# Step sizes of a selective scan made ahead of the scan and kept in DRAM

## The chip, the cores and the metric

The kernel runs on one core of one Trainium2 chip, as one program. The metric is its time on the device in microseconds (us). A core has five engines that run side by side and meet only at semaphores: PE (TensorE, matmul), DVE (VectorE, elementwise and scans), ACT (ScalarE, activation functions), POOL (GpSimd, here elementwise too) and SP (SyncE, which here issues nearly all DMAs). SBUF is the memory in which the arrays lie (one large tensor, `arena`), PSUM (`ps`, eight banks of 512 float32 columns) is what PE writes, DRAM is outside. Each engine works through its own instructions in their written order.

## What is computed

The reference is one block: a group norm, a Mamba-like branch (convolution and a selective scan in four directions) that is added to x, an attention step without softmax, and a mixture of eight experts. The change touches the branch alone:

```python
B_, H_, W_, DM = (4, 32, 32, 384); DI = 192; N = 16; R = 24; K = 4      # 1024 positions per image
xz = _gn(x) @ in_proj_w.T
xh, z = jnp.split(xz, 2, axis=-1)
xc = silu(depthwise_conv3x3(xh) + conv_b)
xs = [xc by rows, xc by columns, and both reversed]                     # K = 4 directions
x_dbl = einsum('bkdl,kcd->bkcl', xs, x_proj_w)
dts, Bs, Cs = jnp.split(x_dbl, [R, R + N], axis=2)
dts = softplus(einsum('bkrl,kdr->bkdl', dts, dt_projs_w) + dt_projs_b)  # the delta of each channel and position
def step(h, inp):
    dA = jnp.exp(d_t[..., None] * As)
    h = h * dA + (d_t * u_t)[..., None] * B_t[:, :, None, :]
    y = jnp.einsum('bkcn,bkn->bkc', h, C_t)
out_y = selective_scan(xs, dts, As, Bs, Cs, Ds)
y = layernorm(sum of the four directions) * silu(z);  return y @ out_proj_w.T
```

## The kernel before

**Tiles.** The four images are worked on in two pairs (`NP` = 2). A tile is 128 partitions (64 channels of both images of a pair) by 1024 positions. There are twelve tiles q (`NQ`: 2 pairs, 2 orders, by rows and by columns, 3 groups of 64 channels), each with two directions, forwards and backwards. A tile and a direction together are a half (24 of them); a half has 16 units, one for each n of the state, so a tile has `UN` = 32 units, and there are 384 in all.

**Prologue.** A loop over the pairs: DVE takes the sums of the group norm of an image, PE adds them over groups and spreads them back, DVE normalises x, PE makes the input projection in three fills of two PSUM banks per image, ACT takes them out (xh into the padded image `xpad`, silu of z into `z_sb`). Then the convolution, three fills per pair: PE does 5 of 9 taps (`PE_TAPS`) with diagonal weights, DVE the other four in `tap_sum` and adds them, ACT applies silu into `xy`, POOL copies the result by columns. A second loop makes the projection `x_proj` for each direction k: ACT copies the rows, and DVE and ACT split B and C into three bfloat16 parts, which SP stores in DRAM (`bc_parts`, `b_rows`, `dt_rows`).

**Scan.** For each unit u: ACT makes the decay, exp(delta * a) (line 624). PE spreads row n of B over the partitions (line 838) and DVE multiplies that by delta * x (line 1235). For 6 of the 16 n (`ON_POOL`) POOL makes this input instead (line 457), from a row of B that SP loads broadcast from `b_rows` into a ring of `XRING` = 2. DVE scans (line 1242). PE spreads the row of C, ACT copies it out of PSUM (line 632), POOL multiplies the states of two units by it (line 476), and PE adds the products up in PSUM, five units later (`LAG`, line 857). At the end of a tile DVE takes the sum out (line 1212).

**The delta** of a half is made while the half ahead of it is scanned. After given n, PE multiplies the rows of dt (line 846), ACT takes it out of PSUM, then Abs, Exp, +1 and Ln (lines 594 to 609); DVE has three steps between them, after n = 7, 10 and 11 (`DELTA_AT`, lines 1195, 1200 and 1205: the part lost in rounding, max(x, 0) + log, and the difference); after n = 12 POOL makes delta * x (line 450, `delta_x`). Only the first half's delta is made ahead of the scan.

**Order.** All of it is written out by hand: what stands behind what in an engine's program, and waits on semaphores. Nothing reorders it. SP too works in order: it waits for what it stores and then issues.

After the scan come the norm over channels, the output projection, attention and the experts, which the change leaves as they are.

## Time and profile before

| | |
|---|---|
| median of 3 runs | 2713.69 us (2710.76 to 2716.58) |
| the profiled execution's own time | 2710.37 us |
| its span, first to last instruction | 2708.6 us |
| mean granted TensorE clock | 0.918 |
| up to the first scan | 0 to 267.22 us |
| scan, to the start of what follows it | 267.22 to 1654.31 us |
| the rest | 1654.31 to 2708.6 us |

In the stretch 260 to 1655 us, DVE is busy 1312.43 us of 1395, POOL 1316.03, PE 1110.14 and ACT 903.03. A busy time says that an instruction was running, not that it got on: an instruction that is held up inside counts as busy. Hence the same instruction is compared in places where its neighbours differ.

### The profile page before, as it was taken

What the parts mean: (1) busy time and instruction counts of PE and PEld (TensorE: products, weight loads), DVE (VectorE), ACT (ScalarE), POOL (GpSimd) and SP (SyncE); (2) the same over time, 40 slices, a digit from 0 to 9 for tenths busy, and PEclk for the clock granted to TensorE, in tenths of its full rate; (3) what the DMA queues carried; (4) which work ended last, traced back from release to release, by engine and by line L of the source; (5) the groups of instructions that cost most, each with busy time, mean ns of one, the idle gap of its engine ahead of it and who ended that gap; (6) DMA issues with size and microseconds to landing.
All of it is one profiled execution on the core that took longest, in us unless ns stands there. A gap on an engine that the chain in (4) does not pass through costs nothing.

```text
span 2708.6 us, 21624 instructions
## 1 busy us (share of the span) xinstructions
PE 2190.3 (81%) x6116; PEld 1001.7 (37%) x6116; DVE 1622.6 (60%) x1337; ACT 1152.9 (43%) x1277; POOL 1446.6 (53%) x503
## 2 busy tenths in 40 slices
PE   3886777788787887887878886679998469999998
PEld 1332233333332333333333332345545335555554
DVE  2433999999999999999999995632221200000000
ACT  1225666666666666666666662211111011211111
POOL 0001899999999999999999993000000321111110
PEclk9987899989999989999989988789999689999999
DMA  5115121212222222121122124001100342222230
GB/s 199 58 23 136 55 54 55 54 54 72 54 55 53 54 72 60 49 62 52 49 61 56 54 55 181 23 35 47 47 14 33 133 156 107 107 106 104 105 105 16
DMA packets 69131, 193.92 MB, mean 72 GB/s; under 512 B 10160, under 2 KB 35875, under 8 KB 67426
## 3 DMA queue, kind: packets, MB, share of 16 engines
q1 hardware_dynamic: 62946, 176.45, 21.3%
q0 software_dynamic: 6144, 16.98, 1.8%
q8 instruction: 19, 0.31, 0.0%
q14 instruction: 22, 0.18, 0.0%
HBM read 154.89 MB, written 40.44 MB: 72 GB/s over the span
## 4 chain that ended last, share of the span: by engine, by line
PE 46%; DVE 22%; issue 17%; POOL 8%; ACT 3%; DMA 1%; SPq 1%; DVEq 1%; POOLq 0%; ACTq 0%
PE ps L1093 9%; PE ps L1081 9%; DVE arena L1242 6%; PE ps L857 6%; DVE ps L1235 5%; POOL arena L476 5%; PE ps L801 3%; DVE arena L1200 3%; PE ps L1045 3%; DVE arena L1195 2%; PE ps L970 2%; PE ps L838 2%; POOL arena L450 2%; PE ps L812 2%; PE ps L846 2%
## 5 line engine op out<-in xcount | busy, mean ns | idle before, releaser
L476 POOL TENSOR_TENSOR arena<-arena 128x2048 f32<-128x2048 f32 x192 | 906.9, 4734 | 40.5 <-DVE arena L1242 39.1
L857 PE MATMUL ps<-arena 128*128 128x512 f32 x1536 | 792.5, 641 | 80.8 <-POOL arena L476 65.5
L1242 DVE TENSOR_TENSOR_SCAN arena<-arena,ps 128x1024 f32<-128x1024 f32 x240 | 548.7, 2286 | 40.9 <-DVE ps L1235 29.7
L632 ACT ACTIVATE arena<-ps 128x1024 f32<-128x1024 f32 x384 | 391.9, 1021 | 357.4 <-PE ps L838 352.4
L838 PE MATMUL ps<-arena 96*128 (+1 forms) x1248 | 375.1, 411 | 205.8 <-DVE arena L1242 165.0
L857 PEld LDWEIGHTS ps<-arena 128*128 128x128 f32 x1536 | 308.1, 204 | 375.0 <-issue 236.0
L457 POOL TENSOR_TENSOR arena<-arena 128x1024 f32<-128x1024 f32 x144 | 362.2, 2516 | 29.1 <-DMA arena<-b_rows 26.9
L1242 DVE TENSOR_TENSOR_SCAN arena<-ps,arena 128x1024 f32<-128x1024 f32 x144 | 327.2, 2272 | 11.1 <-ACT ps L624 10.9
L838 PEld LDWEIGHTS ps<-arena 96*128 96x128 bf16 x1248 | 116.0, 103 | 555.1 <-DVE arena L1242 248.3
L1235 DVE TENSOR_TENSOR ps<-ps,arena 128x1024 f32<-128x1024 f32 x240 | 290.9, 1212 | 20.1 <-PE ps L838 17.6
L1459 DVE TENSOR_TENSOR arena<-ps,arena 128x384 f32<-128x384 f32 x32 | 17.8, 557 | 448.9 <-PE ps L1093 448.9
L624 ACT ACTIVATE arena<-arena 128x1024 f32<-128x1024 f32 x240 | 273.7, 1141 | 2.6 <-DVE arena L1205 2.6
L514 POOL DMA_INDIRECT out<-arena x32 | 31.8, 993 | 435.8 <-DVE arena L1464 435.8
L492 POOL COPY arena<-arena 128x384 f32 x32 | 17.8, 597 | 454.4 <-DVE arena L1364 454.4
L1093 PE MATMUL ps<-arena 128*128 128x384 f32 x768 | 250.1, 486 | 0.0
L1081 PE MATMUL ps<-arena 128*128 128x512 f32 x576 | 248.7, 592 | 0.0
L624 ACT ACTIVATE ps<-arena 128x1024 f32<-128x1024 f32 x144 | 160.8, 1117 | 61.0 <-DVE arena L1242 60.6
L1093 PEld LDWEIGHTS ps<-arena 128*128 128x128 f32 x768 | 145.4, 190 | 101.6 <-issue 3.8
L1081 PEld LDWEIGHTS ps<-arena 128*128 128x128 f32 x576 | 109.6, 191 | 135.8 <-issue 134.0
L748 ACT ACTIVATE arena<-ps,arena 128x512 f32<-128x512 f32 x96 | 66.0, 688 | 175.9 <-PE ps L1081 175.9
L755 ACT ACTIVATE arena<-arena 128x384 f32<-128x384 f32 x32 | 16.7, 523 | 232.3 <-DVE arena L1459 232.3
L443 POOL COPY arena<-arena x6 | 12.4, 2071 | 174.2 <-ACT arena L561 174.2
(167 smaller groups left out, 1891.9 us busy)
## 6 DMA issues: line engine op xcount, KB each, us to landing
arena<-b_rows SPq DMA_DIRECT2D x288, 256.0 KB, 3.9
arena<-in_w SPq DMA_DIRECT2D x16, 2304.0 KB, 13.2
slot_in<-arena SPq DMA_DIRECT2D x8, 772.0 KB, 16.2
arena<-slot_in SPq DMA_DIRECT2D x8, 772.0 KB, 18.0
arena<-in_xT SPq DMA_DIRECT2D x4, 1536.0 KB, 9.4
arena<-in_x_tok SPq DMA_DIRECT2D x1, 6144.0 KB, 21.9
tokens<-arena SPq DMA_DIRECT2D x4, 1536.0 KB, 6.2
out<-arena SPq DMA_DIRECT2D x4, 1536.0 KB, 9.7
```

What stands on the lines that cost most here:

```text
L457: nc.gpsimd.tensor_tensor(xin[:, x % XRING], xin[:, x % XRING], dux[:, dr], ALU.mult).then_inc(in_ok, 1)
L476: nc.gpsimd.tensor_tensor(hst[:, h:h + 2], hst[:, h:h + 2], c_sb[:, c:c + 2], ALU.mult).then_inc(p2_ok, 2)
L624: nc.scalar.activation(dst, dlt[:, dr], ACT.Exp, scale=a_neg[:, q % OJ, dr, n:n + 1]).then_inc(dec_ok, 1)
L632: nc.scalar.activation(c_sb[:, u % RING], C_PS, ACT.Copy).then_inc(c_free, 1)
L801: mm = pe.matmul(SLOT3[n % 3][:, h * 512:(h + 1) * 512], w_in[:, t, r, j], xt[:, r, t, h * 512:(h + 1) * 512], start=(t == 0), stop=(t == ...
L838: mm = pe.matmul(dst[:, h * 512:(h + 1) * 512], sel_lhs[0:BR, n], bc[0:BR, q % OJ // J, dr, m, h * 512:(h + 1) * 512], start=True, stop=True)
L857: mm = pe.matmul(Y_PS[:, h * 512:(h + 1) * 512], ident, hst[:, u % HRING, h * 512:(h + 1) * 512], start=(u == 0), stop=(u == UN - 1))
L1045: pe.matmul(ps[:, 3 + i % 2, 0:C], xnT[:, t, i * P:(i + 1) * P], w_eff[:, t], start=(t == 0), stop=False)
L1081: mm = pe.matmul(ps[:, 3 + m % 3, :], w1[s][:, t, m * P:(m + 1) * P], xeT[:, s, t], start=(t == 0), stop=(t == CT - 1))
L1093: mm = pe.matmul(ps[:, 6 + i % 2, 0:C], h_sb[:, m, i * P:(i + 1) * P], w2[s][:, m], start=(m == 0), stop=(m == MT - 1))
L1235: nc.vector.tensor_tensor(x, x, dux[:, dr], ALU.mult).then_inc(p1_ok, 1)
L1242: nc.vector.tensor_tensor_scan(h, f, x, 0.0, ALU.mult, ALU.add).then_inc(sc_ok, 1)
```

## The change

The deltas and the products delta * x of all 24 halves are made in the prologue, stored in DRAM (`delta`, `delta_x`, 512 KB each per half) and loaded again by SP during the scan, two DMAs per half, after the first scan of the half ahead (`FETCH_AT`). They pass through a ring of `MADE` = 4 buffers `d_mk` and `u_mk`. Per half DVE now has four steps (abs, 1 + u, lost part, add log), ACT three (bias, Exp, Ln) and POOL two (`take_lost`, `delta_x`). The projection of the second pair's input is woven between the steps of the first pair's deltas. The group statistics of all four images are taken early, the first image is loaded ahead of the constants, the convolution has 6 taps on PE, silu of z is applied once per pair, and POOL makes 5 of 16 inputs (n = 1, 4, 7, 10, 13) with a ring of 5.

```diff
-DELTA_AT = (7, 10, 11)
-POOL_AT = 12
-DT_AT = 2
-ACT_AT = (3, 4, 5, 6, 9)
+HALVES = 2 * OJ
+FETCH_AT = 5
-ON_POOL = (1, 4, 6, 9, 12, 14)
+ON_POOL = (1, 4, 7, 10, 13)
-XRING = 2
+XRING = 5
-TAPS, PE_TAPS = 9, 5
+TAPS, PE_TAPS = 9, 6
+MADE = 4
...
         def _(sp):
+            sp.dma_start(xt[:, 0], a["xT"][0]).then_inc(ld_x[0], 16)
...
+            def store_delta(p, i):
+                sp.wait_ge(d_ok, m + 1)
+                sp.dma_start(dl_dram[q * 2 + dr], d_mk[:, m % MADE]).then_inc(dm_st[m % MADE], 16)
+                sp.wait_ge(du_ok, m + 1)
+                sp.dma_start(du_dram[q * 2 + dr], u_mk[:, m % MADE]).then_inc(dm_st[m % MADE], 16)
...
+            for i in range(MADE):
+                sp.wait_ge(dm_st[i], NP * HALVES // MADE * 32)
             for U in range(NQ * UN):
+                if U % N == FETCH_AT and N <= U < (2 * NQ - 1) * N:
+                    half = U // N + 1
+                    sp.wait_ge(sc_ok, U - FETCH_AT + 2)
+                    load_delta(half // 2, half % 2)
                 if U % UN in POOL_UNITS:
                     b_row(U // UN, U % UN)
...
         def _(pool):
+            def take_lost(p, i):
+                m = p * HALVES + i
+                pool.wait_ge(pd_ok, m + 1)
+                nc.gpsimd.tensor_tensor(d_mk[:, m % MADE], d_mk[:, m % MADE], u_mk[:, m % MADE], ALU.subtract).then_inc(d_ok, 1)
+            def delta_x(p, i):
+                nc.gpsimd.tensor_tensor(u_mk[:, m % MADE], d_mk[:, m % MADE], xy[:, q, :], ALU.mult).then_inc(du_ok, 1)
+            for p in range(NP):
                 for j in range(J):
+                    by_columns(p, j)
+                for i in range(HALVES):
+                    take_lost(p, i)
+                    delta_x(p, i)
...
         def _(act):
+            def dt_out(p, i):
+                act.wait_ge(dt_ok, m + 1)
+                if m >= MADE:
+                    act.wait_ge(dm_st[m % MADE], m // MADE * 32)
+                nc.scalar.activation(d_mk[:, m % MADE], DT_PS, ACT.Identity, bias=dt_bias[:, q % OJ, dr, :]).then_inc(dtev_ok, 1)
+                for s in range(HALVES + 2):
+                    if s < HALVES:
+                        dt_out(p, s)
+                    if 1 <= s <= HALVES:
+                        exp_abs(p, s - 1)
+                    if s >= 2:
+                        log_w(p, s - 2)
...
+                if p == 0:
+                    in_proj_out(3, J - 1)
...
         def _(dve):
+            def abs_x(p, i):
+                nc.vector.scalar_tensor_tensor(out=u_mk[:, m % MADE], in0=d_mk[:, m % MADE], scalar=-1.0, in1=d_mk[:, m % MADE],
+                                               op0=ALU.mult, op1=ALU.max).then_inc(ab_ok, 1)
+            def lost_part(p, i):
+                chain.link(nc.vector.tensor_scalar(w, u, 1.0, None, ALU.add))
+                nc.vector.scalar_tensor_tensor(out=u, in0=w, scalar=-1.0, in1=u, op0=ALU.add, op1=ALU.subtract).then_inc(lost_ok, 1)
+            def add_log(p, i):
+                nc.vector.scalar_tensor_tensor(out=d, in0=d, scalar=0.0, in1=w_mk[p][:, m % 2],
+                                               op0=ALU.max, op1=ALU.add).then_inc(pd_ok, 1)
+                for s in range(HALVES + 2):
+                    if s < HALVES:
+                        abs_x(p, s)
+                    if 1 <= s <= HALVES:
+                        lost_part(p, s - 1)
+                    if s >= 2:
+                        add_log(p, s - 2)
+                    k = s // J + 1
+                    if k < K and s % J == 0:
+                        split_rest(p, k)
+                    if k < K and s % J == 1:
+                        split_lo(p, k)
...
-                    if n in DELTA_AT and not (last and dr):
-                        delta(q + dr, 1 - dr, DELTA_AT.index(n))
```

On DVE in the scan, around n = 10 and 11 of a half, there stood before (line 1242 is the scan, printed here by its base form; `b_spread` is the row of B on PE):

```order
L1235 TENSOR_TENSOR ps<-ps,arena 128x1024 [waits b_spread]
L1238 REGISTER_ALU [waits input_ready]
L1242 SCALAR_TENSOR_TENSOR arena<-arena,ps 128x1024 [waits y_added,decay_ready]
L1205 TENSOR_TENSOR arena<-arena 128x1024 [waits delta_uncorrected]
L1228 REGISTER_ALU
L1229 REGISTER_ALU [waits input_on_pool]
```

and now, over one POOL unit and the two units behind it:

```order
L1403 SCALAR_TENSOR_TENSOR arena<-ps,arena 128x1024 [waits y_added,decay_ready,input_on_pool]
L1396 TENSOR_TENSOR ps<-ps,arena 128x1024 [waits b_spread]
L1403 SCALAR_TENSOR_TENSOR arena<-arena,ps 128x1024 [waits y_added,decay_ready,input_ready]
L1396 TENSOR_TENSOR ps<-ps,arena 128x1024 [waits b_spread]
L1403 SCALAR_TENSOR_TENSOR arena<-arena,ps 128x1024 [waits y_added,decay_ready,input_ready]
```

The three steps of a delta are gone from between the scans; one POOL unit is followed by two units whose input DVE multiplies itself.

On DVE in the prologue, one step of the new loop over the halves, with the split of the next direction between steps:

```order
L1293 SCALAR_TENSOR_TENSOR arena<-arena 128x1024 [waits delta_stored1,dt_evacuated]
L1303 TENSOR_SCALAR arena<-arena 128x1024 [waits delta_uncorrected,u_ready]
L1304 SCALAR_TENSOR_TENSOR arena<-arena 128x1024 [waits dve_chain]
L1310 SCALAR_TENSOR_TENSOR arena<-arena 128x1024 [waits ln_ready]
L1284 TENSOR_TENSOR arena<-arena 64x1024 [waits split_mid]
```

and on POOL, where before there were only the six copies by columns ahead of the scan:

```order
L486 COPY arena<-arena 128x1024 [waits slot_free] x3
L492 TENSOR_TENSOR arena<-arena 128x1024 [waits delta_uncorrected]
L500 TENSOR_TENSOR arena<-arena 128x1024 [waits x_by_columns,delta_ready]
```

The DVE rows are abs, 1 + u, lost part, add log and a split; the POOL pair is `take_lost` and `delta_x`, twelve times per pair of images. Work of both engines on SBUF now stands side by side in the prologue.

## Rows read from the trace of the kernel before

**Rows 1.** Busy time of a stretch: window, length, PE, PEld, DVE, ACT, POOL, PEclk, DMA, GB/s

```profile
260.00:1655.00 1395.00, 1110.14 (x2872) 439.58 (x2872) 1312.43 (x708) 903.03 (x907) 1316.03 (x360) 0.92 0.21 56
```

**Rows 2.** Groups of instructions, 230 to 1750 us: busy, mean ns, idle before

```profile
L476 POOL TENSOR_TENSOR arena<-arena 128x2048 f32<-128x2048 f32 x192 | 906.9, 4734 | 40.5 <-DVE arena L1242 39.1 <-issue 1.4
...
L457 POOL TENSOR_TENSOR arena<-arena 128x1024 f32<-128x1024 f32 x144 | 362.2, 2516 | 29.1 <-DMA arena<-b_rows 26.9 <-POOL arena L450 1.5
...
L1235 DVE TENSOR_TENSOR ps<-ps,arena 128x1024 f32<-128x1024 f32 x240 | 290.9, 1212 | 20.1 <-PE ps L838 17.6 <-POOL arena L450 2.5
...
L1200 DVE SCALAR_TENSOR_TENSOR arena<-arena 128x1024 f32<-128x1024 f32 x24 | 69.8, 2910 | 1.1 <-ACT arena L609 1.1
L1195 DVE SCALAR_TENSOR_TENSOR arena<-arena 128x1024 f32<-128x1024 f32 x24 | 66.5, 2769 | 4.6 <-ACT arena L605 4.6
L450 POOL TENSOR_TENSOR arena<-arena 128x1024 f32<-128x1024 f32 x24 | 56.5, 2353 | 71.6 <-DVE arena L1205 71.6
...
L1205 DVE TENSOR_TENSOR arena<-arena 128x1024 f32<-128x1024 f32 x24 | 28.8, 1200 | 0.0
```

**Rows 3.** DVE in order of time, inside a tile: start, us, engine, line

```profile
727.04 1.20 DVE L1235 TENSOR_TENSOR ps<-ps,arena 128x1024 f32<-128x1024 f32 x1
...
730.64 1.21 DVE L1235 TENSOR_TENSOR ps<-ps,arena 128x1024 f32<-128x1024 f32 x1
...
734.25 2.26 DVE L1242 TENSOR_TENSOR_SCAN arena<-ps,arena 128x1024 f32<-128x1024 f32 x1
736.43 1.21 DVE L1235 TENSOR_TENSOR ps<-ps,arena 128x1024 f32<-128x1024 f32 x1
```

**Rows 4.** DVE in order of time: a tile's sum taken out, first and eleventh

```profile
398.12 1.26 DVE L1212 SCALAR_TENSOR_TENSOR arena<-arena,ps 128x1024 f32 x1
...
1553.91 1.25 DVE L1212 SCALAR_TENSOR_TENSOR arena<-arena,ps 128x1024 f32<-128x1024 f32 x1
```

**Rows 5.** POOL in order of time, 696 to 714 us

```profile
696.53 9.98 POOL L476 TENSOR_TENSOR arena<-arena 128x2048 f32<-128x2048 f32 x2
...
708.80 4.52 POOL L476 TENSOR_TENSOR arena<-arena 128x2048 f32<-128x2048 f32 x1
```

**Rows 6.** DVE in the same stretch, in order of time

```profile
698.44 3.69 DVE L1195 SCALAR_TENSOR_TENSOR arena<-arena 128x1024 f32<-128x1024 f32 x1
702.06 1.22 DVE L1235 TENSOR_TENSOR ps<-ps,arena 128x1024 f32<-128x1024 f32 x1
```

**Rows 7.** DVE with POOL idle: the first half's delta, ahead of the scan

```profile
258.58 1.23 DVE L1195 SCALAR_TENSOR_TENSOR arena<-arena 128x1024 f32<-128x1024 f32 x1 [4.56 <-ACT arena L605]
```

**Rows 8.** DVE with POOL idle, in order of time: first sums, and a tap

```profile
25.58 3.65 DVE L1133 BATCH_NORM_STATS2 arena<-arena 128x6 f32<-128x512 f32 x6
...
71.18 0.75 DVE L1167 TENSOR_SCALAR arena<-arena 128x1024 f32<-128x1024 f32 x1 [8.41 <-ACT arena L554]
```

**Rows 9.** PE in the prologue, in order of time: an image's projection, then the convolution

```profile
36.24 18.76 PE L801 MATMUL ps<-arena 128*128 128x512 f32 x36 [2.64 <-DVE arena L1155]
...
80.13 25.92 PE L812 MATMUL ps<-arena 128*128 128x512 f32 x60
```

**Rows 10.** ACT takes the first delta out of PSUM

```profile
254.08 1.11 ACT L594 ACTIVATE arena<-ps,arena 128x1024 f32<-128x1024 f32 x1
```

**Rows 11.** DMAs issued up to 300 us: count, KB each, median us to landing

```profile
arena<-in_xT SPq DMA_DIRECT2D x4, 1536.0 KB, 9.4
z_scratch<-arena SPq DMA_DIRECT2D x4, 768.0 KB, 5.5
...
arena<-b_rows SPq DMA_DIRECT2D x10, 256.0 KB, 3.9
...
arena<-bc_parts SPq DMA_DIRECT2D x2, 768.0 KB, 8.7
...
b_rows<-arena SPq DMA_DIRECT2D x8, 128.0 KB, 2.1
```

**Rows 12.** DVE's first scan

```profile
267.22 2.29 DVE L1242 TENSOR_TENSOR_SCAN arena<-arena,ps 128x1024 f32<-128x1024 f32 x1
```

More of the change, by code:

```diff
@@ L463, in read_outs @@
                     U = q * UN + u
-                    if n == POOL_AT and not (last and dr):
-                        delta_x(q + dr, 1 - dr)
                     for ahead in (u + LEAD, u + LEAD + 1):
@@ new lines, in delta_product @@
+            def delta_product(p, i):
+                k, j, q, dr = half_of(p, i)
+                m = p * HALVES + i
+                pe.wait_ge(rows_ok, p * K + k + 1)
+                if m:
+                    pe.wait_ge(dtev_ok, m)
+                else:
+                    pe.wait_ge(xn_ok, B)
+                for h in range(2):
+                    mm = pe.matmul(DT_PS[:, h * 512:(h + 1) * 512], dt_w[0:DR, q % OJ, dr],
+                                   rows[0:DR, k % 2, h * 512:(h + 1) * 512], start=True, stop=True)
+                mm.then_inc(dt_ok, 1)
@@ new lines, in taps @@
+            def taps(p, j):
+                dve.wait_ge(xh_ok, p * IN_P + (J + j + 1))
+                if p * J + j >= 2:
+                    dve.wait_ge(conv_ok, p * J + j - 1)
+                acc = tap_sum[:, (p * J + j) % 2].rearrange("p (h w) -> p h w", w=HW)
+                for tap in range(PE_TAPS, TAPS):
+                    dy, dx = divmod(tap, 3)
+                    x, w = xpad[:, j, dy:dy + HW, dx:dx + HW], conv_w[:, j, tap:tap + 1]
+                    if tap == PE_TAPS:
+                        ins = nc.vector.tensor_scalar(acc, x, w, None, ALU.mult)
+                    else:
+                        ins = nc.vector.scalar_tensor_tensor(out=acc, in0=x, scalar=w, in1=acc, op0=ALU.mult, op1=ALU.add)
+                    chain.link(ins)
@@ new lines, in _ @@
+            add_taps(0, 2)
+            normalise_x(3)
+            for p in range(NP):
+                if p:
+                    for j in range(J):
+                        taps(p, j)
+                        add_taps(p, j)
+                split_rest(p, 0)
+                split_lo(p, 0)
+                for s in range(HALVES + 2):
[5 more added lines that the diff above has]
+                        add_log(p, s - 2)
+                    k = s // J + 1
+                    if k < K and s % J == 0:
+                        split_rest(p, k)
+                    if k < K and s % J == 1:
+                        split_lo(p, k)
```

617 lines of the change are left out of this document (341 added, 276 removed).

## The prediction, made before the changed kernel was run

> **What bounds the kernel now.** I read the busy times by stretches first. In the scan DVE is busy 1312 us of 1395 and POOL 1316, PE 1110 with its clock at 0.92 (most of the time at 2.4 GHz), ACT 903 [rows 1]: two engines share the bound, and the stretch from the first scan at 267.2 us [rows 12] to its end at 1654.3 is half of the time. So the change is worth what it takes from DVE and POOL there, less what it adds ahead of the first scan, where nothing else runs.
>
> The DVE's own pace comes from the order of time. A unit whose input DVE multiplies takes 727.04 to 730.64, 3.60 us; a unit whose input POOL makes takes 734.25 to 736.43, 2.18 us [rows 3]. From the first sum taken out to the eleventh there are ten tiles, 1155.8 us, 115.6 each [rows 4]. A tile has 20 units of the first kind and 12 of the second (98.2 us), the sum taken out (1.2 from start to start) and the three delta steps of two halves, 2.77 + 2.91 + 1.20 us [rows 2], less 0.07 each where the next instruction starts early (698.44 + 3.69 against 702.06 [rows 6]): 6.67 per half, 13.3 per tile. That makes 112.7, and 2.9 us per tile in which DVE waits, mostly for PE's row of B (17.6 us in all, [rows 2]).
>
> The second thing to see is that DVE and POOL hold each other up. The step of line 1195 takes 1.23 us while POOL is idle [rows 7] and 2.77 on average in the scan [rows 2]. At 698.44 it took 3.69 [rows 6], and POOL's pair of instructions from 696.53 took 9.98 [rows 5], where one of them alone takes 4.52 (708.80, [rows 5]): DVE stood still until the first had ended (about 701.0), ran, and POOL's second began only then. So an instruction of DVE that reads two arrays of SBUF and one of POOL that does so take turns. The scans and line 1235 read one of their arrays from PSUM and show nothing of it: 1.21 us beside POOL [rows 3].
>
> **The change in the scan.** Gone from DVE: the delta steps of 23 halves (the first half's lay ahead of the scan), 23 x 6.67 = 153.4 us. Added: one more unit per half that DVE multiplies, 24 x (3.60 - 2.18) = 34.1 us. Net -119.3 us. Gone from POOL: 23 x 2.35 for delta * x and 24 x 2.36 for the sixth input, and the holding up: line 457 takes 2.516 on average and line 476 4.734 [rows 2], against 2.35 and about 4.5 undisturbed, some 60 us in all. A half costs POOL then 8 x 4.5 + 5 x 2.36 = 48 us, while DVE needs, for the eleven and five units of a half, 11 x 3.60 + 5 x 2.18 + 0.6 = 51.1 us. DVE alone is the bound, and POOL has 3 us of room per half, about what it has now. PE loses the products of dt but gains 24 x 2 spreads; its 1110 us become some 1100 in 1265, hidden. Of DVE's waits, 34 us in all, I take 8 us off, since POOL is later less often; the bounds are 0 and 34. The new loads, 1 MB per half, are issued behind the half's first scan, some 50 us ahead of their use, against landings of 4 to 9 us [rows 11]: nothing. But on SP the rows of B for n = 7 and later stand behind that wait and those two loads. They are used two units later (some 7 us plus POOL's 4.5), and land 3.9 us after issue [rows 11], so they are hidden with some 4 us to spare; if not, see the rivals. Scan: **-127 us**.
>
> **The change in the prologue, up to the first delta.** One image lands ahead of the constants. Two to four images took 9.4 us to landing, 768 KB took 5.5 [rows 11]; I take 8 us instead of the 25.58 at which DVE begins now [rows 8]. From there to PE's first projection are 10.7 us as now (36.24 - 25.58, [rows 8, 9]): 18.7. An image on PE takes 18.8 us with the clock low at first, and 36 passes of 0.43 us, 15.5, with it up [rows 9]; I take 18.8 + 17.4 for the two, and between the fills PE waits for the early statistics, which are now queued in its program; from DVE's 4.8 us of sums per image plus the small steps I reckon 11 us of it: 66. The convolution goes from 5 to 6 taps on PE, 25.92 x 6/5 = 31.1 us [rows 9]: 97. DVE's taps are beside it and do not bind. Then PE makes two fills of the next pair's input and one of x_proj, 12 passes of 0.43 us each (25.92/60), 15.6, and the first product of dt, 1.7; ACT 1.1 [rows 10]: the first delta is out at **115 us**.
>
> **The loop over the deltas.** Per half DVE has abs, lost part and add log at 1.23 [rows 7] and 1 + u at 0.75 [rows 8], POOL two instructions at 2.35 [rows 2]. All read SBUF on both sides. In turns that is 3.69 + 0.75 + 4.70 = 9.14 us, and a split per direction (1.2 us, every third half) makes it **9.55 per half**. I followed one step through: POOL's first, abs, POOL's second, then 1 + u, lost part and add log, which releases POOL again; there is no gap. Beside it PE needs 5.2 us per half, ACT 3.3 to 5. The stores: 512 KB should land in 4.2 us (between 2.1 for 128 KB and 5.5 for 768 KB, [rows 11]). A buffer comes back after four halves, and dt_out waits for it; in the step above that wait is covered by POOL's turn up to a landing of about 8 us.
>
> Before POOL's first turn the loop has to fill. In pair one: x_proj 5.2, product 1.7, input fill 5.2, product 1.7, then ACT 1.1 and DVE 4.4, 19.3 us. Of the 12 x 9.14 + 4 x 1.2 = 114.5 us in turns, 11 have been done by then: the loop ends 19.3 + 103.5 = 123 us after the first delta, at 238. Pair two has no input fills, 14.3 + 103.5 = 118.
>
> **Between the pairs** little overlaps. ACT takes the last input fill out only behind its last log, about 10 us before POOL's end (227.5); the second convolution fill can start at 229.6. DVE's first tap group begins behind its last add log (231) and takes turns with POOL's last three instructions: 241.5. Then its addition 1.2, ACT's silu 1.1, the third fill of PE 10.4, addition and silu 2.3: 256.6. x_proj, copy and split, 9.6: the second loop starts at 266 and ends at 384. Store landed 388.5, product 1.2, first scan 389.9 against 267.2. The second scan needs POOL's input, whose row of B is loaded only behind the last store: 388.5 + 0.4 + 3.9 + 2.4 = 395.2 against 269.4 now, where it followed at once. Prologue: **+126 us**.
>
> **One term rests on no row.** No row here shows a TENSOR_SCALAR of this size beside POOL. I let it take its turn, as its neighbours do, since abs ahead of it and lost part behind it are of the kind that does. At the other end it would be hidden behind POOL's second instruction, 0.75 x 22 = 16 us less. The Trainium skill, page "SBUF — State Buffer", section "Who interferes with whom", states that tensor_scalar from SBUF can run in a mode which uses both ports and then shuts GpSimd out. By that rule the term stays in, and by its opposite the kernel would come to 2693.
>
> **Sum**, against the profiled execution's own 2710.4: -127 + 126 = -1, 2709. The median of the runs is 3.3 above that execution, so on its scale **2712 us**.
>
> **Rivals.** (1) The turns are not fully paid. POOL's pair lost 9.98 - 9.0 = 1.0 us, not 1.23, to one DVE step [rows 5], and 1 + u may be hidden. Then the ring of four buffers bounds the loop: from dt_out to add log 5.9, POOL 4.7, landing 4.2, over two steps 14.8, with the splits 8.0 per half. 22 halves x 1.5 = 33 us less: 2679. For it: the 1.0. Against: the mean of 2.77, which is 1.23 and a wait of half a POOL instruction. (2) Slower: each change between the engines in a step costs a semaphore and a restart that my sum leaves out. Five changes at 0.2 us are 1.0 per half, 22 us: 2734. It decides from 0.3 us per step on. (3) Slower: stores land late, since 1 MB leaves every 9.5 us while SP also stores the parts. Beyond 8 us of landing each us is paid per half; at 9 us (four images took 9.4, a load behind others 8.7 [rows 11]) 22 us: 2734. (4) Slower: the scan waits more, because rows of B come behind the loads of the deltas and PE's lags are no longer hidden by delta steps: 4.5 us per tile instead of 2.2, 27 us: 2739. (5) Faster: DVE's waits in the scan go away with POOL's holding up, 26 us more: 2686. (6) The loads of a delta are late and DVE waits at each half's start: it would cost 23 times; but 50 us of lead speak against it, so I give it no chance of its own.
>
> **Chances.** Forecast 0.27, (1) 0.27, (2) 0.16, (3) 0.08, (4) 0.12, (5) 0.10. A measurement of this kernel can tell 0.2%, 5.4 us, from no change. The forecast's own width is some 8 us each way, which gives 0.06 faster, 0.15 within, 0.06 slower. Faster 0.27 + 0.10 + 0.06 = 0.43; slower 0.16 + 0.08 + 0.12 + 0.06 = 0.42; within 0.15. The range goes from (1), 2679, to (4), 2739, widened by the 1 to 2 us of the runs' spread: 2677 to 2742; two of these cases together could leave it on either side.
>
> **What would show it.** First delta out of PSUM near 115 us; DVE's abs and add log at 1.5 to 3.6 us instead of 1.23 while POOL works; a step of the loop 9.2 to 9.8 us; the first scan near 390. In the scan no instruction of POOL above 4.55 us, a tile in 104 to 105 us instead of 115.6, and DVE's idle time there under 3 us per tile beyond its own 0.2 us handovers. Wrong would be: a first scan before 370 (the turns are cheap) or after 405, a loop step set by the wait for a store, or tiles over 107 us.

## The result: 1.3% faster, and the profile after

The changed kernel took 2675.72 us (2674.89 to 2676.96, 4 runs) beside 2712.23 us for the kernel before (2702.75 to 2716.58, 4 runs): a ratio of 0.987, with 0.9844 to 0.9897 as its 95% interval. The prediction was 2712, no change, with a range of 2677 to 2742; the time lies 1.3 us below its low end. The direction "faster" had been given 0.43.

The profiled execution took 2675.52 us, its span is 2673.7. Its busy times by stretches, for the part ahead of the scan, the scan, and the rest (columns as in [rows 1]):

```profile
0.00:381.70 381.70, 264.21 (x534) 106.17 (x534) 269.01 (x243) 146.94 (x143) 154.78 (x63) 0.79 0.41 145
381.70:1622.00 1240.30, 1024.99 (x2826) 425.53 (x2826) 1176.40 (x659) 785.04 (x763) 1143.11 (x312) 0.94 0.27 71
1622.00:2673.70 1051.70, 897.89 (x2828) 482.93 (x2828) 215.45 (x482) 174.81 (x296) 113.23 (x128) 0.92 0.23 84
```

In the scan DVE is busy 95% of the time and POOL 92%, so DVE alone is the bound now. The groups of instructions that answer to [rows 2] (the whole span; busy, mean ns, idle before with its releasers):

```profile
L531 POOL TENSOR_TENSOR arena<-arena 128x2048 f32<-128x2048 f32 x192 | 869.7, 4530 | 87.0 <-DVE arena L1403 86.8
...
L1396 DVE TENSOR_TENSOR ps<-ps,arena 128x1024 f32<-128x1024 f32 x264 | 319.0, 1208 | 15.5 <-issue 9.9 <-PE ps L957 5.4
...
L514 POOL TENSOR_TENSOR arena<-arena 128x1024 f32<-128x1024 f32 x120 | 283.3, 2361 | 7.9 <-DMA arena<-b_rows 7.9
...
L500 POOL TENSOR_TENSOR arena<-arena 128x1024 f32<-128x1024 f32 x24 | 73.1, 3046 | 1.9
...
L492 POOL TENSOR_TENSOR arena<-arena 128x1024 f32<-128x1024 f32 x24 | 64.5, 2686 | 117.9 <-DVE arena L1310 117.9
L1303 DVE TENSOR_SCALAR arena<-arena 128x1024 f32<-128x1024 f32 x24 | 59.4, 2475 | 0.2
L1293 DVE SCALAR_TENSOR_TENSOR arena<-arena 128x1024 f32<-128x1024 f32 x24 | 51.1, 2128 | 13.8 <-ACT arena L636 13.3
```

POOL's product with C fell from a mean of 4734 ns to 4530, its undisturbed value, and its product with B from 2516 to 2361 (lines 476 and 457 in [rows 2]). The holding up has left the scan. It has gone into the prologue: there the mean of DVE's abs (L1293) is 2.13 us and that of POOL's two (L492, L500) 2.69 and 3.05 instead of 2.35. DVE waited 12.0 us for PE's row of B in the ten tiles of [rows 4], and waits 5.4 now; over the same ten tiles its idle time as a whole is 60.5 us before (1155.8 long, 1095.3 busy) and 48.4 after. The handovers of 0.19 us inside a product unit, which my count of a tile contains, are 39.0 of the 60.5 and 42.9 of the 48.4; so the waits proper fell from some 22 us in ten tiles to 5.6. Of the 22, PE's row made 12.0, and the other 10.0 lay ahead of scans whose input POOL had made, nearly all of it until ACT's decay was ready.

DVE in order of time, the start of its work, the first sum taken out of PSUM and the eleventh, and the scans that start the scan stage:

```profile
7.77 3.66 DVE L1219 BATCH_NORM_STATS2 arena<-arena 128x6 f32<-128x512 f32 x6 [7.77 <-DMA arena<-in_xT]
...
381.68 2.29 DVE L1403 TENSOR_TENSOR_SCAN arena<-arena,ps 128x1024 f32<-128x1024 f32 x1
387.53 2.29 DVE L1403 TENSOR_TENSOR_SCAN arena<-ps,arena 128x1024 f32<-128x1024 f32 x1 [3.56 <-POOL arena L514]
...
496.88 1.25 DVE L1373 SCALAR_TENSOR_TENSOR arena<-arena,ps 128x1024 f32 x1
...
1526.69 1.26 DVE L1373 SCALAR_TENSOR_TENSOR arena<-arena,ps 128x1024 f32<-128x1024 f32 x1
...
1622.10 2.91 DVE L1423 TENSOR_TENSOR arena<-arena 128x512 f32<-128x512 f32 x3
```

A tile takes (1526.69 - 496.88) / 10 = 102.98 us, against 115.58 ([rows 4]). The table sums the span by where it moved (before: 2708.6):

| stretch | before | after | difference | forecast |
|---|---|---|---|---|
| up to the second scan | 269.4 | 387.5 | +118.1 | +126 |
| from there to the end of the scan | 1384.9 | 1234.6 | -150.3 | -127 |
| rest | 1054.3 | 1051.6 | -2.7 | 0 |
| sum | 2708.6 | 2673.7 | -34.9 | -1 |

Both large terms were too pessimistic: the scan by 23 us, the prologue by 8. The 2.7 us of the rest, where the kernels are the same, are traced to nothing. The loop over the deltas, one step of it in order of time (POOL, DVE and one row of ACT):

```profile
163.53 2.37 POOL L492 TENSOR_TENSOR arena<-arena 128x1024 f32<-128x1024 f32 x1 [3.02 <-DVE arena L1310]
163.58 1.11 ACT L636 ACTIVATE arena<-ps,arena 128x1024 f32<-128x1024 f32 x1 [7.08 <-DMA delta_x<-arena]
...
164.72 2.25 DVE L1293 SCALAR_TENSOR_TENSOR arena<-arena 128x1024 f32<-128x1024 f32 x1 [1.28 <-ACT arena L636]
...
165.97 3.21 POOL L500 TENSOR_TENSOR arena<-arena 128x1024 f32<-128x1024 f32 x1
...
166.90 2.83 DVE L1303 TENSOR_SCALAR arena<-arena 128x1024 f32<-128x1024 f32 x1
...
169.77 1.23 DVE L1304 SCALAR_TENSOR_TENSOR arena<-arena 128x1024 f32<-128x1024 f32 x1
170.91 1.22 DVE L1310 SCALAR_TENSOR_TENSOR arena<-arena 128x1024 f32<-128x1024 f32 x1
...
172.21 2.35 POOL L492 TENSOR_TENSOR arena<-arena 128x1024 f32<-128x1024 f32 x1 [3.02 <-DVE arena L1310]
```

Read it as one chain. POOL's first product ends at 165.9, and only then does DVE's abs do its work; its 2.25 us are a wait of 1.2 and 1.1 of work. POOL's second, issued at 165.97, gets its turn when abs is done (166.9) and ends at 169.2; the TENSOR_SCALAR issued at 166.90 takes 2.83 us instead of 0.69 to 0.75. Lost part and add log follow, 1.14 us from start to start, and add log releases POOL at 172.21, 1.30 us behind its own start: 8.68 us without a gap, though POOL shows 3.02 us as idle and DVE's durations are inflated.

### The profile page after: what moved, and what is told of

It is laid out like the page before. It is cut to its first block, busy times and chain, and to the rows that moved or that the text cites. A ratio compares the mean times of both kernels' runs of the same rounds, so it can differ in the third digit from the quotient of the medians.

```text
span 2673.7 us, 21345 instructions
## 1 busy us (share of the span) xinstructions
PE 2187.1 (82%) x6188; PEld 1014.6 (38%) x6188; DVE 1660.9 (62%) x1382; ACT 1106.8 (41%) x1202; POOL 1411.1 (53%) x503
## 4 chain that ended last, share of the span: by engine, by line
PE 44%; DVE 26%; issue 18%; POOL 6%; ACT 4%; DMA 1%; DVEq 1%; ACTq 0%; POOLq 0%; SPq 0%
DVE arena L1403 15%; PE ps L1192 9%; PE ps L1180 9%; PE ps L968 7%; DVE ps L1396 6%; PE ps L957 3%; ACT ps L705 3%; PE ps L1144 3%; POOL arena L500 2%; PE ps L1069 2%; PE ps L880 2%; POOL arena L492 2%; PE ps L867 1%; PE ps L1145 1%; PE ps L1085 1%
## 5 line engine op out<-in xcount | busy, mean ns | idle before, releaser
L531 POOL TENSOR_TENSOR arena<-arena 128x2048 f32<-128x2048 f32 x192 | 869.7, 4530 | 87.0 <-DVE arena L1403 86.8
L968 PE MATMUL ps<-arena 128*128 128x512 f32 x1536 | 768.6, 625 | 29.1 <-DVE arena L1373 25.7
L1403 DVE TENSOR_TENSOR_SCAN arena<-arena,ps 128x1024 f32<-128x1024 f32 x264 | 603.7, 2287 | 44.9 <-DVE ps L1396 24.2
L957 PE MATMUL ps<-arena 96*128 (+1 forms) x1296 | 361.5, 395 | 216.7 <-DVE arena L1403 191.7
L1396 DVE TENSOR_TENSOR ps<-ps,arena 128x1024 f32<-128x1024 f32 x264 | 319.0, 1208 | 15.5 <-issue 9.9
L705 ACT ACTIVATE arena<-arena 128x1024 f32<-128x1024 f32 x264 | 300.7, 1139 | 26.0 <-DVE arena L1403 22.2
L514 POOL TENSOR_TENSOR arena<-arena 128x1024 f32<-128x1024 f32 x120 | 283.3, 2361 | 7.9 <-DMA arena<-b_rows 7.9
L1403 DVE TENSOR_TENSOR_SCAN arena<-ps,arena 128x1024 f32<-128x1024 f32 x120 | 271.8, 2265 | 3.6 <-POOL arena L514 3.6
L1180 PE MATMUL ps<-arena 128*128 128x512 f32 x576 | 248.6, 593 | 0.0
L705 ACT ACTIVATE ps<-arena 128x1024 f32<-128x1024 f32 x120 | 134.0, 1117 | 106.9 <-DVE arena L1403 106.9
L492 POOL TENSOR_TENSOR arena<-arena 128x1024 f32<-128x1024 f32 x24 | 64.5, 2686 | 117.9 <-DVE arena L1310 117.9
L913 PE MATMUL ps<-arena 48*128 48x512 f32 x96 | 68.9, 854 | 53.9 <-ACT arena L636 52.7
## 6 DMA issues: line engine op xcount, KB each, us to landing
slot_in<-arena SPq DMA_DIRECT2D x8, 772.0 KB, 13.9
```

Source lines behind the costliest of these rows:

```text
L492: nc.gpsimd.tensor_tensor(d_mk[:, m % MADE], d_mk[:, m % MADE], u_mk[:, m % MADE], ALU.subtract).then_inc(d_ok, 1)
L514: nc.gpsimd.tensor_tensor(xin[:, x % XRING], xin[:, x % XRING], dux[:, dr], ALU.mult).then_inc(in_ok, 1)
L531: nc.gpsimd.tensor_tensor(hst[:, h:h + 2], hst[:, h:h + 2], c_sb[:, c:c + 2], ALU.mult).then_inc(p2_ok, 2)
L705: nc.scalar.activation(dst, dlt[:, dr], ACT.Exp, scale=a_neg[:, q % OJ, dr, n:n + 1]).then_inc(dec_ok, 1)
L957: mm = pe.matmul(dst[:, h * 512:(h + 1) * 512], sel_lhs[0:BR, n], bc[0:BR, q % OJ // J, dr, m, h * 512:(h + 1) * 512], start=True, stop=True)
L968: mm = pe.matmul(Y_PS[:, h * 512:(h + 1) * 512], ident, hst[:, u % HRING, h * 512:(h + 1) * 512], start=(u == 0), stop=(u == UN - 1))
```

## The experiments

Twelve kernels were run. Times of the kernel before in the same jobs were 2713.49, 2711.17 and 2713.14 us. The changed kernel was not run again in these jobs, and the kernel before moved by 2.3 us between them, so a difference of 2 or 3 us between two medians below says nothing. "First scan" is the start of DVE's first scan, "tile" the mean over the ten tiles between the first and the eleventh sum.

| kernel | us (ratio to before, interval) | first scan | tile |
|---|---|---|---|
| before | 2712.23 | 267.2 | 115.6 |
| after | 2675.72 (0.987, 0.9844 to 0.9897) | 381.7 | 103.0 |
| before_pool5 | 2736.34 (1.0085, 1.0068 to 1.0102) | 269.0 | 117.4 |
| after_pool6 | 2648.03 (0.9757, 0.9741 to 0.9774) | 381.8 | 100.6 |
| after_two_sbuf | 2840.68 (1.0466, 1.0449 to 1.0484) | 381.4 | 117.2 |
| after_one_sbuf | 2761.72 (1.0177, 1.016 to 1.0194) | 381.8 | 110.4 |
| after_xring2 | 2672.84 (0.9857, 0.984 to 0.9874) | 381.9 | 102.6 |
| all_dve | 2639.11 (0.9733, 0.9717 to 0.975) | 344.1 | 103.0 |
| abs_act | 2659.5 (0.9808, 0.9792 to 0.9825) | 367.2 | 102.8 |
| after_stores_twice | 2680.81 (0.9888, 0.9867 to 0.9909) | 386.3 | 102.8 |
| abs_act_stores_twice | 2672.89 (0.9855, 0.9835 to 0.9875) | 379.9 | 102.8 |
| taps5 | 2675.55 (0.9873, 0.9856 to 0.989) | 381.0 | 102.8 |
| all_dve_taps5 | 2634.89 (0.9721, 0.9701 to 0.9742) | 341.2 | 102.9 |
| abs_act_all_dve_pool6 | 2603.65 (0.96, 0.9575 to 0.9624) | 335.9 | 100.6 |

### The scan: where did DVE's waits go?

**The sixth input of POOL, apart from the deltas.** The kernel before with the changed kernel's share of POOL, and the changed kernel with the old share (there with rows of B in a ring of four, since six does not divide by five):

```diff
-ON_POOL = (1, 4, 6, 9, 12, 14)
+ON_POOL = (1, 4, 7, 10, 13)      # before_pool5; after_pool6 has the lines the other way round
```

> The kernel before with POOL making 5 of 16 inputs (n = 1, 4, 7, 10, 13) in place of 6; nothing else. DVE gets 24 more products, 24 x 1.42 = 34 us; POOL loses 24 x 2.5 = 60 us. The question is why DVE's waits in the scan, 2.9 us per tile before, have gone in the changed kernel. Theory B, POOL's load: they go here too, 34 us less, and the time stays near 2712 (tile 115.6). Theory A, DVE's steps with two SBUF arrays hold POOL up, and theory D, PE's and ACT's delta steps stand between the units: the waits stay, tile 118.4, time near 2745.

> The changed kernel with POOL making 6 of 16 inputs as before (n = 1, 4, 6, 9, 12, 14), its ring of B rows 4 long. DVE saves 34 us; per half it needs 49.7 us, POOL 8 x 4.52 + 6 x 2.36 = 50.3. Theory B (the waits went with the sixth input): they come back, 34 us, and the time stays near 2676. Theory A (they went because nothing holds POOL up): POOL becomes the bound by a hair, tile 100.6 to 101.5 instead of 103.0, time 2648 to 2658.

The kernel before becomes 23 us slower with five inputs: it loses two pool units and gains two product units per tile, 2.84 us, and gets 1.8. So of the 2.9 us by which its tile exceeded my count the sixth input made 1.1. The trace says more than the tile. DVE's scans of an input made by POOL and its products, in ten tiles, with their idle time at the end of the row; first the kernel before, then this one:

```profile
L1242 DVE TENSOR_TENSOR_SCAN arena<-ps,arena 128x1024 f32<-128x1024 f32 x121 | 274.9, 2272 | 10.0 <-ACT ps L624 9.9
L1235 DVE TENSOR_TENSOR ps<-ps,arena 128x1024 f32<-128x1024 f32 x200 | 242.4, 1212 | 12.0 <-PE ps L838 12.0
```

```profile
L1242 DVE TENSOR_TENSOR_SCAN arena<-ps,arena 128x1024 f32<-128x1024 f32 x101 | 229.3, 2270 | 3.2 <-ACT ps L624 0.5
L1235 DVE TENSOR_TENSOR ps<-ps,arena 128x1024 f32<-128x1024 f32 x220 | 266.8, 1213 | 2.2 <-PE ps L838 2.1
```

The two together fell from 22.0 us to 5.4, what the changed kernel has (5.6), although the delta steps are still in this kernel's scan and POOL's product with C is still held up to 4740 ns. So taking the sixth input off POOL removes DVE's idle time, and the holding up alone doesn't make it. (The edit moves the places of the inputs as well, from n = 6, 9, 12, 14 to 7, 10, 13; load and places weren't separated.) What this kernel's tile still has above my count, 1.8 us, lies for the most part inside the delta steps: line 1200 now takes 3.72 us on average instead of 2.94, line 1195 2.46 instead of 2.82, and the six steps of a tile 14.8 us instead of 13.9.

The changed kernel gains 28 us with six. Its scan then has POOL busy nearly throughout:

```profile
L531 POOL TENSOR_TENSOR arena<-arena 128x2048 f32<-128x2048 f32 x192 | 868.5, 4534 | 10.0 <-DVE arena L1403 10.0
```

POOL's idle time ahead of its product with C fell from 87.0 to 10.0 us, and still its instructions take 4.53. With POOL that full, DVE's waits for PE's row are back at 11.8 us in ten tiles (5.6 in the changed kernel). So the part of the change that hands an input back to DVE costs this kernel 28 us. What pays for it is the move of the deltas out of the scan.

**What a step on DVE costs in the scan.** Three instructions per half put into the changed kernel's scan, 69 in all, as the kernel before has three delta steps. Their results are not used. One kernel reads two arrays of SBUF, the other one array, in two bn_stats of 512 columns:

```diff
+if n in (7, 10, 11) and not (last and dr):        # after_two_sbuf
+    nc.vector.scalar_tensor_tensor(out=scratch, in0=dlt[:, dr], scalar=-1.0, in1=dux[:, dr], op0=ALU.add, op1=ALU.subtract)
+    for hh in range(2):                           # after_one_sbuf, instead
+        nc.vector.bn_stats(scratch[:, hh], dlt[:, dr, hh * 512:(hh + 1) * 512])
```

> The changed kernel with three more DVE instructions per half in the scan, after n = 7, 10 and 11 (23 halves): scalar_tensor_tensor of two SBUF arrays of 1024 columns into a scratch tile that nobody reads. PE, ACT, SP and POOL have nothing new. Theory A: each costs DVE 1.2 us of its own and 0 to 2.5 us of standing behind POOL, and holds POOL up by 1; per half near the 6.7 us of the kernel before, and waits of DVE for PE return: +160 to +190 us, 2835 to 2865, POOL's line 531 at 4.7 us on average. Theories B and D: only the instructions' own length, +83 us, 2759.

> The same at the same places with instructions that read one SBUF array: two bn_stats of 512 columns for each, 1.2 us together, into a scratch tile that nobody reads. DVE's own time grows by 23 x 3 x 1.2 = 83 us, nothing takes turns with POOL. All theories: +75 to +85 us, 2751 to 2761, POOL's line 531 still 4.53. What after_two_sbuf costs above this one is the price of taking turns.

The two differ by 79.0 us, or 1.14 per step, about half of a POOL instruction of 2.35 or a quarter of one of 4.5. POOL's groups in the trace of the first and of the second:

```profile
L532 POOL TENSOR_TENSOR arena<-arena 128x2048 f32<-128x2048 f32 x192 | 908.0, 4729 | 212.0 <-DVE arena L1404 199.9 <-ACT arena L711 11.1 <-issue 0.3
```

```profile
L532 POOL TENSOR_TENSOR arena<-arena 128x2048 f32<-128x2048 f32 x192 | 869.7, 4530 | 172.9 <-DVE arena L1404 169.8 <-issue 0.4
```

POOL's mean goes back to 4729 ns, the 4734 of [rows 2], for the instruction that reads two arrays, and stays at 4530 for the pair that reads one: the holding up works in both directions, and it isn't a matter of how much work DVE has. The two steps also differ in what they write, 1024 columns against a few numbers; that difference wasn't tested apart, and the loop below has an instruction with a single SBUF array that does take a turn. So "two arrays of SBUF" is the kind of step that was tested, not a proven boundary.

A tile of after_two_sbuf takes 117.2 us, near the 117.4 of before_pool5, which has the real delta steps with PE's and ACT's share. The agreement is in part chance, since the parts differ: the six steps take 13.8 us per tile here and 14.8 there, and DVE waits 11.0 us for PE's row in ten tiles here and 2.2 there. That PE's and ACT's share costs nothing is better seen in before_pool5 itself, whose 5.4 us of waits are no more than the changed kernel's. The waits for PE's row nearly double with any step put in (9.9 us in after_one_sbuf, 5.6 without); the turns add 1.1 to that. Why they do wasn't traced.

**The rows of B.** A ring of two rows instead of five (`XRING = 2`):

> The changed kernel with a ring of 2 rows of B for POOL's inputs, as before, instead of 5. Theory C (the waits in the scan went because the rows come early): POOL waits for rows again, 0.5 to 1 us each in places, and DVE's waits return in part, +15 to +30 us, 2690 to 2706. Theories A and B: POOL has room, nothing, 2674 to 2680.

No loss; the median is 2.9 us lower, which is not to be told from no change. With two rows POOL does wait for them, 9.3 us in the whole scan against 0.3 with five, and its slack takes it. The fourth rival, that rows of B come late behind the loads of the deltas, has nothing left.

### The loop over the deltas: turns or ring?

**Without POOL.** Lost part and delta * x are computed by DVE:

```diff
# DVE, add_log, behind the old last instruction
+dve.wait_ge(pd_ok, m + 1)
+nc.vector.tensor_tensor(d, d, u_mk[:, m % MADE], ALU.subtract).then_inc(d_ok, 1)
...
+dve.wait_ge(d_ok, m + 1)
...
+nc.vector.tensor_tensor(u_mk[:, m % MADE], d, xy[:, q, :], ALU.mult).then_inc(du_ok, 1)
# POOL
-for i in range(HALVES):
-    take_lost(p, i)
-    delta_x(p, i)
```

> The changed kernel with both of POOL's instructions in the delta loop (take_lost, delta_x) made by DVE right behind add log. DVE then has six instructions per half, 1.0 + 0.6 + 1.15 + 1.2 + 1.2 + 1.2 = 6.5 us with its hand-over waits about 6.8, and POOL none. Theory 'turns': step 8.67 becomes 6.8, 22 x 1.9 = 41 us less plus the two loops' tails, 2625 to 2640. If DVE and POOL truly worked side by side, moving POOL's 4.7 us onto DVE (4.4 us of its own) would make the step 8.5 to 9 us: no gain, 2674 to 2690.

Giving DVE 50% more instructions made the first scan come 37.6 us earlier. One step of the loop, DVE in order of time:

```profile
177.72 1.23 DVE L1290 SCALAR_TENSOR_TENSOR arena<-arena 128x1024 f32<-128x1024 f32 x1
178.86 0.69 DVE L1300 TENSOR_SCALAR arena<-arena 128x1024 f32<-128x1024 f32 x1
179.58 1.23 DVE L1301 SCALAR_TENSOR_TENSOR arena<-arena 128x1024 f32<-128x1024 f32 x1
180.72 1.22 DVE L1307 SCALAR_TENSOR_TENSOR arena<-arena 128x1024 f32<-128x1024 f32 x1
181.97 1.23 DVE L1310 TENSOR_TENSOR arena<-arena 128x1024 f32<-128x1024 f32 x1
183.24 1.23 DVE L1315 TENSOR_TENSOR arena<-arena 128x1024 f32<-128x1024 f32 x1
```

Two instructions that took POOL 4.7 us take DVE 2.5, and in turns nothing is hidden behind the other engine anyway. The TENSOR_SCALAR takes 0.69 here, against 2.83 beside POOL.

**Without abs on DVE.** ACT takes the absolute value, right behind dt_out, and DVE's instruction is gone:

```diff
+nc.scalar.activation(u_mk[:, m % MADE], d_mk[:, m % MADE], ACT.Abs).then_inc(ab_ok, 1)
...
-if s < HALVES:
-    abs_x(p, s)
```

> The changed kernel with the absolute value in the prologue's delta loop made by ACT from d_mk instead of DVE. The changed kernel's trace shows steps of 8.67 us in which DVE and POOL run one after the other without a gap: POOL 2.35, abs 1.0, POOL 2.35, 1 + u 0.6, lost part 1.15, add log 1.2. Theory 'turns' (this sum is the bound): 22 to 24 steps get 1.0 us shorter, 2650 to 2656. Theory 'ring' (dt_out waits for the store of four halves ago, and that wait is the bound): the chain from dt_out on stays as long, 2674 to 2680.

The first scan comes 14.5 us earlier; the turn of 1.0 to 1.15 us on 22 halves would have been 22 to 25, and the time, 2659.5, lies between what the two theories had expected. The step is 7.7 us (mean start to start of dt_out, third to twelfth half) instead of 8.46, and ACT waits for a buffer:

```profile
162.17 1.11 ACT L636 ACTIVATE arena<-ps,arena 128x1024 f32<-128x1024 f32 x1 [5.24 <-DMA delta_x<-arena]
```

In the changed kernel ACT waits for the same DMA (7.08 at 163.58, above), so that the wait alone doesn't tell whether it binds. Doubling the stores does.

**The stores twice.** Each delta and delta * x is stored a second time to a spare place, and a buffer comes free when all four transfers have landed, in the changed kernel and in abs_act:

```diff
+sp.dma_start(spare[q * 2 + dr, 0], d_mk[:, m % MADE]).then_inc(dm_st[m % MADE], 16)
+sp.dma_start(spare[q * 2 + dr, 1], u_mk[:, m % MADE]).then_inc(dm_st[m % MADE], 16)
```

> The changed kernel, with each delta and delta * x stored a second time to a spare place in DRAM, and each buffer released only when all four transfers have landed (2 MB per half instead of 1 MB). The prediction said that a landing is covered by POOL's turn up to some 8 us, and that its third rival costs 1 us per half for each us beyond. A 512 KB store landed in 2.6 to 2.7 us, so four should be down by 6 or 7 us after POOL's product. Theory 'turns' (DVE and POOL, in turns, set the loop; the ring of four buffers has room): first scan stays at 382 +- 3 us and the time at 2676 +- 5. Theory 'ring' (the wait for the stores is already near binding): about half of the extra 3 us on each of 22 halves, first scan near 410 and the time near 2705. Result does not depend on the spare copies.

> The same doubled stores in the kernel in which ACT takes the absolute value (its first scan is at 367.2 us, its time 2659.5; there ACT was seen waiting up to 5.4 us for the store of delta * x). Theory 'ring' for this kernel (with abs off DVE the wait for the buffers binds, at least in part): up to 1.3 us more on each of 22 halves, first scan 380 to 396, time 2673 to 2688, while the changed kernel without that edit stays where it is. Theory 'handover' (the rest of what removing abs should have given is lost in waits of DVE for ACT, not in the ring): first scan stays within 3 us of 367 and the time within 5 of 2660.

The median times to landing in the first of the two:

```profile
spare<-arena SPq DMA_DIRECT2D x48, 512.0 KB, 4.1
delta<-arena SPq DMA_DIRECT2D x24, 512.0 KB, 2.6
delta_x<-arena SPq DMA_DIRECT2D x24, 512.0 KB, 2.6
```

The 4.1 mixes two kinds: one by one, the first spare store of a half lands in a median of 3.6 us and the second in 4.4. The second is issued 0.84 us behind the store of delta * x (161.45 and 160.61 in that trace), so a buffer comes free some 0.8 + 4.4 - 2.6 = 2.6 us later. In the changed kernel this cost 4.7 us in the first scan (386.3), 0.2 per half, a little outside the 3 us that I had allowed; in abs_act it cost 12.7 (379.9), 0.6 per half, just under the range that the ring theory gave. So in the changed kernel the turns bind and the ring does so in a few steps only; once a turn is taken out, the ring is next. The middle ground between the two expectations for abs_act is this.

### The prologue: one tap moved back to DVE

```diff
-TAPS, PE_TAPS = 9, 6
+TAPS, PE_TAPS = 9, 5
```

> The changed kernel with 5 of the 9 taps on PE, as before, instead of 6. PE's convolution is three fills of 10.3 us per pair, DVE's taps lie beside it. If PE sets the pace there: 6 x 1.72 = 10 us less, of which the first fill of pair two is hidden, 2666 to 2668. If DVE's fourth tap, taking turns with POOL at the border of the pairs, is late instead: up to 2 us of that is lost, 2668 to 2672.

> All steps of a delta on DVE (2639.1 us, first scan 344.1), and besides one tap of the convolution moved back from PE to DVE (5 taps on PE as in the kernel before). In the changed kernel the same move gained 6.7 us up to the first delta and lost all of it by the first scan; I put that down to DVE's taps taking turns with POOL at the border of the pairs. If that is the cause, nothing of it is left here: first scan 334 +- 4 (6.7 us of the first pair and about 5 of the second, less some us where DVE's own taps become the bound), time 2627 to 2634. If the cause is another (DVE's own extra tap, or ACT and the queue of fills), first scan 341 to 346 and time 2636 to 2642.

In taps5 the first delta came out at 111.2 us instead of 117.95, and the first scan at 381.0 instead of 381.7: what the first pair gained, the second lost, and the time is 3.5 us above all that I had expected. I took it for the turns with POOL at the border of the pairs, where the first group of taps does suffer:

```profile
218.60 2.83 DVE L1264 TENSOR_SCALAR arena<-arena 128x1024 f32<-128x1024 f32 x1
221.47 9.83 DVE L1266 SCALAR_TENSOR_TENSOR arena<-arena 128x1024 f32<-128x1024 f32 x3
231.34 1.23 DVE L1272 TENSOR_TENSOR ps<-ps,arena 128x1024 f32<-128x1024 f32 x1
232.48 0.74 DVE L1264 TENSOR_SCALAR arena<-arena 128x1024 f32<-128x1024 f32 x1
233.25 5.47 DVE L1266 SCALAR_TENSOR_TENSOR arena<-arena 128x1024 f32<-128x1024 f32 x3
```

That theory doesn't carry it. Without POOL in the loop the same edit moved the first scan by 2.9 us (344.1 to 341.2) and not by 10. At the border of all_dve_taps5 DVE goes through its three groups of taps with no gap:

```profile
214.73 0.74 DVE L1261 TENSOR_SCALAR arena<-arena 128x1024 f32<-128x1024 f32 x1
215.51 5.47 DVE L1263 SCALAR_TENSOR_TENSOR arena<-arena 128x1024 f32<-128x1024 f32 x3
221.01 1.23 DVE L1269 TENSOR_TENSOR ps<-ps,arena 128x1024 f32<-128x1024 f32 x1
```

A group is 0.78 + 5.50 + 1.14 = 7.4 us, and with two taps instead of three (4.17, the changed kernel's) it would be 1.3 less. In the first pair the taps run beside PE's slower fills and do not bind; in the second DVE comes straight from its last add log, and they do. From its first tap to its last addition this kernel loses 2.6 us against all_dve, two groups' worth; in the third all_dve had waited for PE. In taps5 it is 3.95 us, and 3.3 of them lie in the first group, where a third tap alone is 1.3: the other 2.0 I put down to turns with POOL.

The rest is on PE. With a tap less PE stands idle longer ahead of the projection that follows, and makes it at a lower granted clock: the same twelve passes in the changed kernel (clock 1.00) and in taps5 (0.75):

```profile
251.05 5.42 PE L898 MATMUL ps<-arena 128*128 128x512 f32 x12 [2.54 <-ACT arena L613]
```

```profile
248.60 7.25 PE L898 MATMUL ps<-arena 128*128 128x512 f32 x12 [5.98 <-ACT arena L613]
```

That is 1.8 us. Without POOL the pair is 6.91 us (0.78) and 8.21 (0.66), 1.3. So of the 6 us that taps5 lost, about a third each goes to DVE's own extra tap, to the turns and to the clock.

### Everything that helped, together

abs on ACT, lost part and delta * x on DVE, six inputs on POOL:

> The three things that helped, together: absolute value on ACT, lost part and delta * x on DVE (no POOL in the loop over deltas), and six of sixteen inputs made by POOL in the scan (rows of four). DVE then has four instructions of 0.6 to 1.25 us per half and the split, 4.7 us; PE's products and fills take 5.2 per half and are the bound, at 5.3 to 5.7 us per half against 6.65 with all on DVE. Theory 'gains add up': first scan 344 - 24 = 320 +- 5, scan shorter by 27.7 as measured with six inputs alone, time 2639 - 24 - 28 = 2587 +- 8. Theory 'ring' (buffers wait for stores at this pace, 1 MB per 5.5 us): step stays at 6.5 or above, first scan 340 to 346, time 2608 to 2614.

2603.65 us, 4% below the kernel before and the best of the series. The tile is 100.6, as with six inputs alone, and from the first scan on the stage is 25 us shorter than the changed kernel's. The loop is the part that missed: the mean step is 6.28 us in the first pair (7.06 with all on DVE) and the first scan comes at 335.9, between the 320 of "gains add up" and the 340 of "ring". DVE still waits for ACT there and ACT for buffers:

```profile
183.67 1.11 ACT L633 ACTIVATE arena<-ps,arena 128x1024 f32<-128x1024 f32 x1 [2.91 <-DMA delta_x<-arena]
...
186.85 0.69 DVE L1304 TENSOR_SCALAR arena<-arena 128x1024 f32<-128x1024 f32 x1 [1.09 <-ACT arena L642]
```

How much of this is the ring and how much ACT's queue, which now holds four instructions per half, wasn't separated. A larger ring wasn't tried.

## Why the prediction was wrong, point by point

**What bounds the kernel before**: right. DVE and POOL share the bound, and the turns are real: the measured price, 1.14 us per step, agrees with what the three delta steps had over 1.23 us in [rows 2], 1.54, 1.68 and nothing, 1.07 on average.

**The scan, -127 against -150**: the step that failed is "Of DVE's waits, 34 us in all, I take 8 us off". The work removed and added was sized right (a tile's count went from 112.7 to 102.2), but what a tile has above its count fell from 2.9 us to 0.8, 25 us in twelve tiles rather than 8. Some 20 of the 25 are idle time in the profile (22.0 us in ten tiles against 5.6); the rest lies inside busy time. That the idle time goes with the sixth input of POOL is shown: before_pool5, where only POOL's inputs are changed, has 5.4. Not only the waits for PE's row went, which I had looked at, but as many microseconds ahead of the scans of POOL's inputs, which I hadn't. I had written "since POOL is later less often" and given it 8 us without following it through; how a late POOL reaches PE's row and ACT's decay wasn't traced. Rival (5), given 0.10, came near with 26 us, but for a cause that is largely another: it said "with POOL's holding up", and in before_pool5 POOL is held up and the waits are gone. The remaining 6 us lie in the first tile: it took 128.7 us from the second scan to its sum before, 13 more than the mean, and 109.4 after, 6 more; this was not taken apart. PE was busy for 1025 us instead of some 1100, hidden as forecast.

**Up to the first delta, 115 against 117.95**: the parts held (bn_stats at 7.8 for 8, the convolution 31.07 for 31.1). 117.95 is where ACT's instruction starts; my 115 had its 1.1 us in it, so that the delta is out at 119.06, 4 us late. The convolution started at 68.2 instead of 66; the fills and the product behind it took what I had given them and were done at 116.65, and ACT was then in a copy of the split until 117.92:

```profile
116.87 1.05 ACT L628 ACTIVATE arena<-arena 64x1024 bf16<-64x1024 f32 x1
```

**The loop, 9.55 us per half**: the mechanism was right, the size of its terms off. The eighth step behind POOL's second take of the lost part, in order of time:

```profile
145.15 2.36 POOL L492 TENSOR_TENSOR arena<-arena 128x1024 f32<-128x1024 f32 x1 [2.30 <-DVE arena L1310]
...
216.56 2.35 POOL L492 TENSOR_TENSOR arena<-arena 128x1024 f32<-128x1024 f32 x1 [3.02 <-DVE arena L1310]
```

These eight steps, two of them with a split, took 71.4 us, where my terms give 8 x 9.14 + 2 x 1.2 = 75.5. I had summed durations (1.23 and 0.75), while a step is made of starts: about 1.0, 0.6, 1.1 and 1.3 for DVE's four instructions. In the scan I had taken such an overlap off, 0.07 each, and here I had not. The first pair's loop took 118.7 us (first dt_out to POOL's end at 236.6) instead of 123, the second's 116.6 instead of 118. Between them lay 24.3 us instead of 28, and behind them 10.0 instead of 11.2, since the stores landed in 2.6 us and not in 4.2. With the 3 us from 115 to 117.95 that makes -7.6.

**The term without a row**: it stands. TENSOR_SCALAR beside POOL takes 2.83 us against 0.69 alone; it waits for POOL's turn to end, and had it been hidden, as at the other end of my bounds, 13 to 16 us would be missing. The Trainium skill, page "SBUF — State Buffer", section "Who interferes with whom", states that `tensor_scalar` can enter a mode that contends with GpSimd, and that whichever of the two comes second is blocked. This case's trace agrees, with DVE's instruction as the second.

**The rivals.** (1), turns not fully paid and the ring as the bound: the time it gave (2679) is near, but for another reason. The turns are paid in steps without a gap; with the stores doubled the ring cost only 4.7 us. (2), handovers: refuted, the step has no gap. (3), late stores: refuted at 2.6 us; but the margin that I claimed, no cost up to 8 us of landing, was too wide, since at 5.2 us behind the issue of delta * x it already costs 0.2 per half. (4), late rows of B: refuted by after_xring2. Of the signs that I had named, the tile (103.0 for 104 to 105), the step (8.7, and 8.9 with the splits, for 9.2 to 9.8) and the first scan (381.7 for 390) all missed on the fast side. Two errors in the same direction added up: 23 us in the scan and 8 in the prologue, where the range had been made to reach to the largest single case. How near the low end the time came is luck: the 3.3 us that I added to get from a profiled execution to the median were 0.2 in the changed kernel, and the 2.7 us of the rest come from a stretch that the change leaves as it is.

## What to carry to other kernels

When two engines take turns, sharing a chain between them hides nothing, and giving one engine the whole chain can beat it: add up both engines' instructions in start-to-start times and compare with one engine doing all. When a change takes load off an engine that others wait for, list the waits of the bound engine ahead of every kind of instruction, not the largest alone, and test the load by itself with one edit; here that one edit to the kernel before would have shown the missing waits before the change was built. And a range should add the errors that point the same way, not only list them as rivals.
